# The third phase of a decoder kernel: turned scores follow the scores by four slots instead of three

## The reference, cut to what matters

```python
def _L1_attn_ref(x, mask, Wq, Wk, Wv, gq, bq, gk, bk, Wo, bo):      # "self" below
    q = _layernorm(heads(x @ Wq.T), gq, bq); k = _layernorm(heads(x @ Wk.T), gk, bk); v = heads(x @ Wv.T)
    scores = jnp.where(causal, jnp.einsum('nhld,nhmd->nhlm', q, k), NEG)
    return merge(softmax(scores) @ v) @ Wo.T + bo

def _L1_xattn_ref(q, k, v, W_proj, b_proj):                          # "local" below: k = v = context
    scores = jnp.einsum('bhqd,bhkd->bhqk', heads(q), heads(k)) / np.sqrt(8)
    scores = jnp.where(abs(i - j) > 64, -inf, scores)
    return merge(softmax(scores) @ heads(v)) @ W_proj.T + b_proj

x = x + _L1_attn_ref(_layernorm(x), ...)
x = x + _L1_xattn_ref(_layernorm(x), ctx_1024, ctx_1024, ...)
x = x + _L1_ffn_ref(_layernorm(x), ...)      # fake-quantised x @ w.T + bias
```

## Time and profile before

| | |
|---|---|
| median of 3 runs | 1501.81 us |
| the profiled execution, its own time | 1492.6 us |
| its span (first to last instruction) | 1490.9 us |
| mean granted TensorE clock | 0.931 |
| TensorE matmul busy | 1312.9 us (88%) |
| VectorE, ScalarE, GpSimd busy | 1090.7, 1007.4, 631.2 us |

### The profile page before, as it was taken

How to read it: one execution, slowest core, us unless ns; L and a number is a source line. 1 busy time by engine, 2 the same in 40 slices (tenths; PEclk the granted TensorE clock), 3 DMA queues, 4 the chain that set the end, 5 groups by cost and what they waited for, 6 DMA issues and landing times.

```text
span 1490.9 us, 42244 instructions
## 1 busy us (share of the span) xinstructions
PE 1312.9 (88%) x14969; PEld 944.5 (63%) x14969; DVE 1090.7 (73%) x2570; ACT 1007.4 (68%) x2781; POOL 631.2 (42%) x842
## 2 busy tenths in 40 slices
PE   4368999999999999999967999788989989898885
PEld 1125666666666666777757998556666666665564
DVE  6998889999998988876663445357677777666664
ACT  2128999999999999999954565345555564654652
POOL 0012424443534443211035363358666574644653
PEclk9999999999999999999988999678789898989995
DMA  6942242423232242020113332211111110100100
GB/s 142 246 115 54 53 93 51 116 56 88 70 85 51 55 105 51 13 83 13 40 58 99 93 91 60 93 35 35 40 31 50 30 49 25 37 28 25 34 19 15
DMA packets 91500, 94.24 MB, mean 63 GB/s; under 512 B 17696, under 2 KB 78752, under 8 KB 86816
## 3 DMA queue, kind: packets, MB, share of 16 engines
q1 hardware_dynamic: 85344, 82.35, 21.1%
q0 software_dynamic: 4096, 8.40, 2.0%
q10 hardware_dynamic: 1856, 0.79, 0.2%
HBM read 64.76 MB, written 17.83 MB: 55 GB/s over the span
## 4 chain that ended last, share of the span: by engine, by line
PE 58%; DVE 14%; ACT 10%; issue 8%; POOL 4%; DMA 3%; SPq 2%; ACTq 0%; DVEq 0%; POOLq 0%
PE P L794 6%; PE P L956 6%; PE P L2144 6%; PE P L1598 4%; PE P L1631 4%; ACT pr L1017 4%; PE P L812 3%; PE P L938 3%; PE P L2207 3%; PE P L915 3%; PE P L2162 3%; PE P L910 3%; PE P L926 2%; DVE mx L2424 2%; SPq L1450 2%
## 5 line engine op out<-in xcount | busy, mean ns | idle before, releaser
L2424 DVE TENSOR_REDUCE mx<-P 128x8 f32<-128x1024 f32 x128 | 156.6, 1224 | 147.0 <-PE P L2144 86.4
L2336 ACT ACTIVATE et<-P 128x1024 f32<-128x1024 f32 x128 | 131.1, 1024 | 173.8 <-PE P L2151 163.7
L1017 ACT ACTIVATE pr<-P,nm 128x256 f32<-128x256 f32 x512 | 238.6, 499 | 6.5 <-DVE nm L1218 6.4
L1218 DVE TENSOR_REDUCE nm<-P 128x4 f32<-128x1024 f32 x128 | 156.2, 1220 | 26.0 <-PE P L794 24.4
L794 PE MATMUL P<-kt_w,qt 64*128 64x256 f32 x1024 | 145.5, 403 | 4.6 <-ACT pr L1017 4.5
L999 ACT COPY ptS<-P 128x512 f32<-128x512 f32 x256 | 138.0, 598 | 6.6 <-PE P L812 6.3
L990 ACT ACTIVATE pr<-pr,ri 128x256 f32<-128x256 f32 x254 | 119.5, 536 | 25.0 <-DVE pr L1191 24.2
L1691 ACT ACTIVATE hT<-P,mixing 128x128 f32<-128x128 f32 x284 | 81.2, 368 | 71.7 <-PE P L1598 70.9
L702 POOL TENSOR_TENSOR kv_qk<-kv_qk,mixing 128x512 f32<-128x512 f32 x48 | 61.0, 1270 | 152.6 <-DVE pr L1191 152.6
L696 POOL TENSOR_TENSOR kv_qk<-kv_qk,r_w 128x512 f32<-128x512 f32 x48 | 60.9, 1270 | 145.5 <-DVE pr L1191 100.1
L1017 ACT ACTIVATION_READ_ACCUMULATOR pr<-P,nm 128x1 f32 x512 | 118.3, 231 | 0.0
(11 more groups left out here) (334 smaller groups left out, 3627.2 us busy)
## 6 DMA issues: line engine op xcount, KB each, us to landing
kv_qk<-scr_v SPq DMA_DIRECT2D x16, 1024.0 KB, 8.1
r_w<-scr_r SPq DMA_DIRECT2D x16, 1024.0 KB, 11.0
xt<-scr_xs SPq DMA_DIRECT2D x71, 64.0 KB, 2.1
scr_ys<-yt SPq DMA_DIRECT2D x71, 64.0 KB, 1.5
qTe<-packedE SPq DMA_DIRECT2D x256, 8.0 KB
x<-in_x SPq DMA_DIRECT2D x8, 256.0 KB, 10.6
scr_v<-mixing SPq DMA_DIRECT2D x8, 256.0 KB, 2.6
scr_r<-mixing SPq DMA_DIRECT2D x8, 256.0 KB, 2.0
```

Of the source, the lines that this page charges most:

```text
L1017: e = nc.scalar.activation(pr[:, s % 3, h * KEYS:(h + 1) * KEYS], scores(s)[:, h // 2, (h % 2) * KEYS:(h % 2 + 1) * KEYS], ACT.Exp, bias=n ...
L1218: nc.vector.tensor_reduce(nm[:, s % 3, 0:4].rearrange("p (a h) -> p a h", a=2), scores(s).rearrange("p a (h k) -> p a h k", k=KEYS), AX.X, ...
L2336: nc.scalar.activation(et[:, u % 4, :, :, :], scoresT, ACT.Exp).then_inc(S["h_exp"], 1)
L2424: nc.vector.tensor_reduce(mx[:, n % 2, 8 * r:8 * r + 8].rearrange("p (k a) -> p k a", k=2), scores, AX.X, ALU.max, negate=True).then_inc(S ...
```

## The change

The distance between the scores of a unit and its turned scores becomes a constant `LAG` of 4, where 3 stood in the numbers. Everything behind the turned scores keeps its distance to them: values in slot u+6 where it was u+5, transposed back u+7 (u+6), turned again u+8 (u+7), output projection and residual u+9 (u+8). The tables of slots move what needs the finished residual (the "ft" and "quant" steps, and the norms and queries of the edge groups) by one slot, and the loop is one slot longer. The steps of the tables `SELF`, the local queries of the middle groups and the transposes of the maxima stay in their slots. No computation is added or left out.

```diff
-         **{f"ft_stat{b}": 10 + 2 * b for b in range(GS)}, "ft_eps0": 12, "ft_nm0": 13, "ft_eps1": 16, "ft_nm1": 17,
-         "quant0": 18, "quant1": 20, "quant2": 21, "quant3": 23, "ft_bias": 19, "ft": 24, "fmm": 25, "sum": 25, "store": 26}
+         **{f"ft_stat{b}": 11 + 2 * b for b in range(GS)}, "ft_eps0": 13, "ft_nm0": 14, "ft_eps1": 17, "ft_nm1": 18,
+         "quant0": 19, "quant1": 21, "quant2": 22, "quant3": 24, "ft_bias": 20, "ft": 25, "fmm": 26, "sum": 26, "store": 27}
...
-                          for name, at in (("e_stat", -6), ("e_nm", -5), ("v", -2))},
-              "e0": -4, "e1": -2, "e2": 0, "e3": 2, "ft_eps0": 15, "ft_nm0": 16}
+                          for name, at in (("e_stat", -5), ("e_nm", -4), ("v", -2))},
+              "e0": -3, "e1": -1, "e2": 1, "e3": 3, "ft_eps0": 16, "ft_nm0": 17}
...
-FIRST_H, LAST_H = -2, UNITS_H + 21
+LAG = 4
+FIRST_H, LAST_H = -2, UNITS_H + 22
...
                     if 0 <= n < UNITS_H // 2:
                         pe.wait_ge(S["h_max"], 2 * n + 2)
-                        if n >= 2:
-                            pe.wait_ge(S["h_ot"], 2 * n - 3)
+                        if 2 * n > LAG:
+                            pe.wait_ge(S["h_ot"], 2 * n - LAG)
...
-                    u = s - 3
+                    u = s - LAG
                     if 0 <= s < UNITS_H:
...
-                    u = s - 5
+                    u = s - LAG - 2
                     if 0 <= u < UNITS_H:
                         local, g, b, r = unit(u)
                         pe.wait_ge(S["h_sel"], u + 1)
...
-                    u = s - 6
+                    u = s - LAG - 3
...
-                    u = s - 7
+                    u = s - LAG - 4
                     if 0 <= u < UNITS_H and u % 2:
...
-                    u = s - 8
+                    u = s - LAG - 5
                     if 0 <= u < UNITS_H and u % 2:
```

More of the change, by code:

```diff
@@ L2032, in pool_program @@
                             pool.wait_ge(S["d_cmb"], 2 * (at - GS) + 2)
-                            if 0 <= s - 3 < UNITS_H:
-                                pool.wait_ge(S["h_st"], s - 2)
+                            if 0 <= s - LAG < UNITS_H:
+                                pool.wait_ge(S["h_st"], s - LAG + 1)
                             else:
@@ L2197, in tensor_program @@
                         pe.wait_ge(S["h_q2"], min(s, UNITS_H) // 2)
-                        if s >= 9:
-                            pe.wait_ge(S["h_oth"], min(s - 7, UNITS_H) // 2)
+                        if s >= LAG + 6:
+                            pe.wait_ge(S["h_oth"], min(s - LAG - 4, UNITS_H) // 2)
                         if local:
@@ L2227, in tensor_program @@
                         pe.wait_ge(S["h_on"], n + 1)
-                        pe.wait_ge(S["h_ot"], min(s - 5, UNITS_H))
+                        pe.wait_ge(S["h_ot"], min(s - LAG - 2, UNITS_H))
                         if n:
```

## The result

After the change the kernel takes 1778.47 us (median of 4 runs, 1769.73 to 1786.37) beside 1500.06 us for the kernel before in the same comparison: a ratio of 1.181 [1.174, 1.187], slower by some 278 us. The forecast was 1610 and its range ended at 1662. The profiled execution took 1786.37 us, its span is 1784.4 us and the mean granted clock 0.811.

The account below looks back on a forecast made before the run. Slots were taken as set by score matmuls, VectorE's 1.23 us maxima and, in odd slots, the copy `ot`; 88 + 30 + 4 + 4 + 0 - 10 = 116 on 1492.6 gave 1608.6, forecast 1610, range 1558 to 1662.

Parts of the forecast that it names:

- the clock: -10: Third phase: less idle time in TensorE, so fewer slots at the lower clock; -10 us (-30 to +20).
- The two units share stretches of rows, 16 steps in place of 8: Score and turned-score matmuls queue on two stretches of 32 partitions; 8 more steps, 0.89 us higher clock, 1.70 lower.
- 0.88 a slot at the higher clock: Third phase: a pair of slots goes from 6.41 to 8.17 us; 100 slots x 0.88 = 88 us.
- Slots at the lower clock +1.5: Third phase, TensorE the bound: 1.3 to 1.7 us more a slot, 1.5 taken; 20 slots, 30 us.
- The DMA waits go: TensorE's 4.5 us of waits, in 6 places, for the maxima's DMA disappear; at most 12 us won.
- One more drain slot +4, slots 4 to 7 +4: One extra slot of 4.07 us in the drain, +4; slots ahead of 991 us at clock 0.60, +4.
- Uneven VectorE slots 0 (-15 to +15): VectorE's moved steps lengthen some slots and relieve others; 0 us in sum, -15 to +15.
- Slot 56: VectorE gets all its slot 55 work here, the maxima apart; 5.7 us, 2 over the new even slot.
- the clock falls for good: Rival: half the array rows count as little activity, most slots run at 1.2 GHz; some 1775 us, chance 4%.

Follow-up runs that it names:

- e1: Kernel after, with turned scores reading the other half's partitions so scores and turned scores lie on four different stretches of rows; 1541.92 us, ratio 1.022.
- e11: Kernel after, complete, with units changing halves so that units four apart lie on different stretches of rows; 1546.85 us, ratio 1.022.
- e5: Kernel after, with the two full-width mask matmuls of each slot issued twice; 1711.2 us, ratio 1.135.
- e13: Kernel after, with the two full-width mask matmuls of each slot issued three times; 1690.06 us, ratio 1.125.
- e6: Kernel before, with the two full-width mask matmuls of each slot issued twice; 1513.54 us, ratio 1.002.
- e12: Kernel before, with full-width matmuls whose results nothing reads added only where TensorE would wait; 1489.73 us beside 1503.69, ratio 0.990.
- e8: Kernel before, with each pair of turned matmuls issued twice, without any sharing of rows; 1631.69 and 1686.38 us, 1659.04 in the middle.
- e10: Kernel before, with VectorE computing each slot's row maxima twice and the matmuls untouched; 1653.88 us, ratio 1.097.
- e2: Kernel before, distance of three slots, with turned scores reading the other half's partitions so they share the scores' stretches; 1729.18 us, ratio 1.146.
- e4: Kernel after, with all eight score matmuls of a slot issued ahead of the eight turned ones; 1774.65 us, ratio 1.177.

## Why the prediction was wrong

The sharing of the rows, its 8 more steps and their cost at the higher clock were right. What failed is the term "the clock: -10" of the sum, in its sign and not only in its size. By the prediction's own steps:

- *The two units share stretches of rows, 16 steps in place of 8*: right. The records go two at a time, and e1 and e11 take the sharing away and with it 232 to 237 us. By the 3.07 times that the Trainium skill ("TensorE: Matmul & The Clock Gate", Part 3, "Measured speedup vs the span model") gives for four row tiles, two tiles against four would cost 54% of those steps, an estimate. The trace differs: a step of 0.111 us starts four records in e11 and two in the kernel after, the full factor of two.
- *0.88 a slot at the higher clock*: right. Measured (8.15 - 6.41)/2 = 0.87, with `ot` in odd slots 0.41 later as forecast (0.42).
- *Slots at the lower clock +1.5*: too small. Measured 1.94 (even) and 2.30 (odd). TensorE is the bound there, so all 8 steps count, 1.70; I had let the last two hide behind VectorE as they do at the higher clock. The even slot has the output projection (0.43 us in slot 120) where a transpose stood (0.21 in slot 54). The odd slot waits for `ot`, 0.72 us in slot 95, where slot 55 of before was busy throughout.
- *The DMA waits go*: right, and worth as little as said.
- *One more drain slot +4, slots 4 to 7 +4*: behind the last full slot the execution takes 6.0 us more (48.5 against 42.5), ahead of slot 8 it is 5.7 us later.
- *Uneven VectorE slots 0 (-15 to +15)*: -20. By the two levels (below) the waits that are left in slots 8 to 126 fell from some 47 us to some 26. Slot 56, for which I wrote 5.7 us, took 6.68, but not for VectorE's sake: it ran at the lower clock, where 6.68 is any even slot, and VectorE was busy for 4.82 of it beside a TensorE busy throughout.
- *The clock*: the failed step. I reasoned that the clock had fallen behind idle time and that more matmul time leaves less of that. The idle time did shrink (90% to 96% busy), and the lower level grew from 95 to 548 us, some 175 us of the time where the sum had -10. The reading behind it was too narrow as well. Of the ten falls in slots 8 to 126 before, all had 1.0 us or more of idle TensorE in their slot and the one ahead, but only four had 2 or more. After the change 21 of 24 falls had under 1 us there, and two had none, one of them at 1180.4 us above.

The sum again with what was measured: 548.1/7.07 = 77.5 slots at the lower level and 41.5 at the higher; before 94.7/4.94 = 19 and 100.

| term | us |
|---|---|
| 41.5 slots at the higher level x 0.87 | 36 |
| 19 slots that were at the lower level already x 2.13 | 41 |
| 58.5 slots that fell from 3.20 to 7.07 | 226 |
| uneven slots | -20 |
| ahead of slot 8, behind slot 126 | 12 |
| together (1786.4 - 1492.6 = 293.8) | 295 |

In the prediction the first two lines were 118 and the third was -10. Of the 226, 51 are the 0.87 that these slots would have got anyway; 175 are the clock.

The rival "the clock falls for good" had the event and, at 1775 us, the time. Its sum of 743 us for the slots equals the measured one by luck: it had all 119 slots at the lower level with 1.5 added to each, while 77.5 were there with 2.13. Nor did it fall for good: it came back for a slot or two over and over. What was held against it, that clean slots had kept the higher level and the new ones had more matmul time, is what the runs overturn. The Trainium skill says in "TensorE: Matmul & The Clock Gate", "Why this matters for your kernels", to leave no long idle gaps between bursts of matmuls if the clock is to stay up. Here that is not enough: slot 96 was busy 6.89 of 6.89 us and stood at the lower level, and at 1180.4 us the clock fell with no gap before it.

**What is shown of the clock, and what isn't.** Shown: more full-width matmuls raise it, in e5, e13, e6 and, by little and less surely, in e12; more narrow matmuls lower it (e8), longer waits lower it (e10), and the same matmuls two at a time lower it (e2 against before, after against e11). What it is in the narrow matmuls that the clock answers to was not taken apart: no run varied their rows, their columns or their type by themselves. The new order's own 36 to 37 us (e1, e11) were not taken apart either; the later `ot` and the clock (61 to 79 us more at the lower level) are both in them. A distance of five slots, in which parities differ again, was not tried.

## What to carry to other kernels

Narrow matmuls run side by side only while they lie on different stretches of 32 rows, so a change of distance between two interleaved streams must be read for which rows meet, before any wait that it may save. Where part of a phase already runs at the lower clock, the clock isn't a correction to the sum but its largest open term: the range must reach to the case in which most slots fall, however busy the engine is. A few full-width matmuls into a free bank, placed where the engine would wait, are worth a try: here they gave 1% (e12).

## What the runs showed that I had not expected

- A TensorE that is busy nearly all the time can stay mostly at 1.2 GHz: 240.72 of 250 us busy at a mean clock of 0.55 in the kernel after.
- Adding matmuls to the bounding engine made the kernel after faster, 1778 to 1711 and 1690 us with one and two more pairs of masks in a slot, and cost the kernel before 3 us, within the noise, where 51 were added.
- Sixteen records alone on two stretches take 1.16 us at the higher clock (e4) and 2.08 us at the lower (the drain), and a slot's 32 on the same two stretches 2.1 and 3.8 us: the steps simply add.
